# One signal of TensorE a pass, x transposed three pairs ahead, and evenly spaced indirect transfers in a recurrent mixture-of-experts kernel

## The reference

```python
x = L0_attn_x; xn = _layernorm(x)
# branch 1: recurrence, from a second layernorm of xn
u = xn2 @ Ws.T + bs + xn2 @ Wi.T + bi
h_t = tanh(h_{t-1} @ A.T + u_t)                     # a scan over 2048 steps
s = (H @ Wo.T + bo) * sigmoid(xn2 @ Wg.T + bg) + xn
# branch 2: top 4 of 16 experts, each silu(gate) * up, 256 -> 2*128 -> 256
scores = sigmoid(xn @ gate_w.T); idx = top_k(scores + gate_b, 4)
y = sum_k w_k * expert_k(xn) + shared_expert(xn)
out = x + s * silu(y)
```

## Time and profile before

| | |
|---|---|
| time, median of 3 runs | 443.7 us (442.36 to 444.87) |
| span of the profiled execution | 513.9 us |
| busy in it: PE, PEld | 339.1 us (66%), 261.7 us (51%) |
| busy in it: DVE, ACT, POOL | 311.1 us (61%), 251.0 us (49%), 265.4 us (52%) |
| moved by DMA | 109.27 MB, mean 213 GB/s |

### The profile page before, as it was taken

One profiled execution on the slowest core, in us unless ns is written; L12 is line 12 of the kernel. 1 busy time (PEld: TensorE's weight loads), 2 busy tenths in 40 slices (PEclk: granted clock), 3 DMA queues, 4 the chain that ended last, 5 costly groups with the idle time before them and its releaser, 6 DMA issues.

```text
span 513.9 us, 10001 instructions
## 1 busy us (share of the span) xinstructions
PE 339.1 (66%) x3107; PEld 261.7 (51%) x3107; DVE 311.1 (61%) x977; ACT 251.0 (49%) x462; POOL 265.4 (52%) x278
## 2 busy tenths in 40 slices
PE   0365566849467786976799968797876968645210
PEld 0352443626355665755698846575654756433100
DVE  4899776676703545545643626786776555346745
ACT  1851666536434455443787746565664644422000
POOL 2005377766646566655600165766555554436773
PEclk9976698797876889888999989999997898676555
DMA  7998499425443566654779768899977777436653
GB/s 247 305 328 281 129 343 331 161 86 201 143 165 127 175 186 201 196 172 156 216 220 269 227 192 268 281 282 285 285 243 211 249 217 225 128 119 194 174 160 126
DMA packets 88675, 109.27 MB, mean 213 GB/s; under 512 B 9649, under 2 KB 78002, under 8 KB 88626
## 3 DMA queue, kind: packets, MB, share of 16 engines
q1 hardware_dynamic: 74656, 74.47, 45.7%
q0 software_dynamic: 12288, 33.57, 20.7%
q10 hardware_dynamic: 1682, 0.59, 0.4%
HBM read 55.91 MB, written 52.69 MB: 211 GB/s over the span
## 4 chain that ended last, share of the span: by engine, by line
PE 35%; another core or an unknown queue 12%; issue 10%; ACT 8%; DVE 6%; POOL 5%; DMA 1%; ACTq 1%; POOLq 0%; DVEq 0%
PE bank L850 13%; PE bank L872 8%; PE bank L656 6%; POOL xn_parts L638 5%; PE bank L863 3%; ACT xn_f L1851 3%; PE bank L898 2%; ACT sh_h L1868 1%; ACT y_ring L1875 1%; ACT xn_f L1859 1%; ACT x_ring L1881 1%; PE bank L948 1%; DVE mix_sb L1371 1%; PE bank L774 1%
## 5 line engine op out<-in xcount | busy, mean ns | idle before, releaser
L638 POOL DMA_INDIRECT xn_parts<-y_slots,slot_u x128 | 127.2, 994 | 126.2 <-PE bank L656 39.6
L619 POOL DMA_INDIRECT x_slots<-xn_parts,slot_u x128 | 131.7, 1029 | 115.1 <-DVE slot_u L1253 36.0
L850 PE MATMUL bank<-w_all,xn_f 128*128 (+1 forms) x864 | 122.2, 295 | 22.2 <-issue 11.5
L850 PEld LDWEIGHTS bank<-w_all,xn_f 128*128 128x128 f16 x864 | 87.3, 106 | 44.8 <-issue 30.6
L1524 DVE SCALAR_TENSOR_TENSOR xn_f<-bank,xn_f 128x256 f32<-128x256 f32 x72 | 30.5, 424 | 111.9 <-ACT xn_f L1859 69.3
L1851 ACT ACTIVATE xn_f<-bank 128x1024 f16<-128x1024 f16 x72 | 73.5, 1022 | 36.7 <-remote 22.3
L872 PE MATMUL bank<-w_all,sh_silu 128*128 (+1 forms) x432 | 68.2, 299 | 5.5 <-ACT y_ring L1875 4.2
L1875 ACT ACTIVATE y_ring<-bank 128x512 f32<-128x512 f32 x72 | 42.9, 596 | 54.4 <-PE bank L872 33.7
L1859 ACT ACTIVATE xn_f<-bank 128x256 f32<-128x256 f32 x72 | 27.5, 382 | 55.0 <-remote 32.4
L656 PE MATMUL bank<-ident_h,w_stage 128*128 128x128 f16 x576 | 48.6, 231 | 1.5 <-issue 1.4
L872 PEld LDWEIGHTS bank<-w_all,sh_silu 128*128 128x128 f16 x432 | 41.8, 106 | 14.5 <-issue 7.5
(11 more groups left out here) (215 smaller groups left out, 456.9 us busy)
## 6 DMA issues: line engine op xcount, KB each, us to landing
w_stage<-x_slots SPq DMA_DIRECT2D x72, 256.0 KB
y_slots<-y_ring SPq DMA_DIRECT2D x72, 256.0 KB
x_slots<-zero_h SPq DMA_DIRECT2D x10, 1024.0 KB
x_ring<-in_x SPq DMA_DIRECT2D x32, 256.0 KB
w_stage<-in_w13t SPq DMA_DIRECT2D x17, 256.0 KB
x_ring<-in_x SPq DMA_DIRECT2D x8, 512.0 KB, 7.7
out<-mix_sb SPq DMA_DIRECT2D x15, 256.0 KB
w_stage<-in_w2t SPq DMA_DIRECT2D x17, 128.0 KB
```

What stands on the lines that cost most here:

```text
L619: eng.indirect_dma_start(out=x_slots, out_offset=bass.IndirectOffsetOnAxis(ap=slot_u[:, n * TOPK + k:n * TOPK + k + 1], axis=0), in_=xn_pa ...
L638: eng.indirect_dma_start(out=fin_y[:, r, j, k, :], out_offset=None, in_=y_slots[0:2 * READY_PAIR[c] * P, :], in_offset=bass.IndirectOffset ...
L850: mm = eng.matmul(gu[:, j * 2 * F:(j + 1) * 2 * F], xg_T[:, n % 2, ((j * 2 + px) * KD + k) * P:((j * 2 + px) * KD + k + 1) * P], weights_o ...
```

## The change

**Signals.** The signals `pair_t`, `pair_gu`, `pair_ht`, `pair_down`, `scan_mm` and `mix_mm` are gone. The last PE instruction of a pass gives the one signal `pair_pass`, and every engine that waited for a group now waits for the end of its pass (`passed_after`). The shared expert's second product keeps its own signal only in the tail.

**Order in a pass.** PE's pass n is now: first product of pair n+1, transposes of x of pair n+3, transposes of the hidden values of pair n-1, one step of the recurrence, second product of pair n-3. There are 75 passes. ACT and DVE start their pass n with what PE's pass n has finished. The recurrence takes passes 1 to 10 and 12 to 27, a step in each, with a shift in 11 and 28; check, fallback, parts and states move from slots 50, 54, 55 and 86 to 85, 90, 91 and 110, the mixing from slot 93 to slot 123. `UNIT_PAIR` has nine units, in passes 42 to 68, so units 9 to 15 come in the tail. SP loads six pairs ahead.

**Spacing.** In place of the half pairs, POOL writes a small tile (`spacer`, 128 x 128 fp16) before each of the scatters 61 to 127 and each gather of units 0 to 10 and waits for that write: 67 + 88 = 155 times. The gathers of units 11 to 15 have nothing between them.

```diff
-    XB_RING, YS_RING, AHEAD = 6, 5, 5
+    XB_RING, YS_RING, AHEAD = 6, 5, 6
+    X_AHEAD, H_BEHIND, DOWN_BEHIND = 3, 1, 3
...
-        SCAN0 = [6, 24]
-        SHIFT = {21: 0, 48: 1}
+        SCAN_PASS = (1, 2 + WARM)
+        SHIFT_PASS = tuple(first + steps for first, steps in zip(SCAN_PASS, STEPS))
...
-        UNIT_PAIR = tuple(40 + 10 * c // 3 for c in range(10))
+        UNIT_PAIR = tuple(42 + 10 * c // 3 for c in range(9))
...
-        MIX_SLOT = {93 + 6 * c: c for c in range(NU)}
+        MIX_SLOT = {123 + 6 * c: c for c in range(NU)}
...
+            def space(i):
+
+                eng.memset(spacer[:, :], 0.0).then_inc(spaced, 1)
+                eng.wait_ge(spaced, i + 1)
...
                 elif i >= HEAD_SCATTERS:
-                    half_pair(SCATTER_HALF + int((i - HEAD_SCATTERS) / PER_HALF_SCATTER))
+                    space(i - HEAD_SCATTERS)
...
-                    beside_gather(c * FT * TOPK + i)
+                    if c < NU - ROW_UNITS:
+                        space(TOPK * NT - HEAD_SCATTERS + c * FT * TOPK + i)
...
-            for n in range(NPAIR + 2):
-                if n + 2 < NPAIR:
-                    pair_x(n + 2)
+            for n in range(PASSES_OF_PAIRS):
                 beside(SLOTS * n)
                 if n + 1 < NPAIR:
-                    pair_up(n + 1)
+                    last = pair_up(n + 1)
                 beside(SLOTS * n + 1)
-                if 1 <= n <= NPAIR:
-                    pair_h(n - 1)
+                if n + X_AHEAD < NPAIR:
+                    last = pair_x(n + X_AHEAD)
+                if 0 <= n - H_BEHIND < NPAIR:
+                    last = pair_h(n - H_BEHIND)
                 beside(SLOTS * n + 2)
-                if n >= 2:
-                    pair_y_down(n - 2)
+                if (step := scan_place(n)) is not None and n > 1:
+                    last = scan_step(*step)
+                if n in SHIFT_PASS:
+                    scan_shift(SHIFT_PASS.index(n))
+                if n >= DOWN_BEHIND:
+                    last = pair_y_down(n - DOWN_BEHIND)
+                last.then_inc(pair_pass, 1)
```

More of the change, by code:

```diff
@@ L206, in recurrent_gated_moe @@
         zero_e = sb("zero_e", [P, E])
+        spacer = sb("spacer", [P, SPACER], f16)
         lnw_sb, lnb_sb = sb("lnw_sb", [P, KD]), sb("lnb_sb", [P, KD])
@@ L379, in recurrent_gated_moe, with mix_pass, scan_place @@
         UNIT_SLOT = {SLOTS * p: c for c, p in enumerate(UNIT_PAIR)}
-        MIX_SLOT = {93 + 6 * c: c for c in range(NU)}
+        MIX_SLOT = {123 + 6 * c: c for c in range(NU)}
         def mix_place(slot, offset):
             return MIX_SLOT.get(slot - offset)
-        def scan_place(slot):
+        def mix_pass(c):
+            return next(slot for slot, unit in MIX_SLOT.items() if unit == c) // SLOTS
+        def scan_place(n):
             for p in range(2):
-                at_ = slot - SCAN0[p]
-                if 0 <= at_ < STEPS[p] // 2 * 3 and at_ % 3 < 2:
-                    return p, at_ // 3 * 2 + at_ % 3
+                if 0 <= n - SCAN_PASS[p] < STEPS[p]:
+                    return p, n - SCAN_PASS[p]
             return None
@@ L834, in pair_x @@
                     eng.wait_ge(xT_lo, NB)
-                transposed(n % 2, lambda j: x_blk[:, xb_at(n), j // 4, (j % 4) * P:(j % 4 + 1) * P], 8, pair_t)
+                tb = TP[n % 2][:, :].bitcast(f16)
+                for j in range(8):
+                    t = eng.transpose(tb[:, j * P:(j + 1) * P], x_blk[:, xb_at(n), j // 4, (j % 4) * P:(j % 4 + 1) * P],
+                                      ident_h[:, :])
+                return t
             def pair_up(n):
@@ L959, in beside @@
                     experts(EXPERT_SLOT[slot])
-                if (place := scan_place(slot)) is not None:
-                    scan_step(*place)
-                if slot in SHIFT:
-                    scan_shift(SHIFT[slot])
-                if slot == CHECK:
+                if slot == FLAG:
                     scan_check()
@@ L974, in _ @@
             pair_x(0)
-            pair_x(1)
+            pair_x(1).then_inc(pair_pass, 1)
             eng.wait_ge(scored, NB)
@@ L1675, in _ @@
             pair_up(0)
-            for n in range(NPAIR + 2):
-                if (step := scan_place(SLOTS * n)) is not None:
+            pair_split(0)
+            for n in range(PASSES_OF_PAIRS):
+                beside(SLOTS * n)
+                if (step := scan_place(n)) is not None:
                     scan_sum(*step)
-                beside(SLOTS * n)
-                if (step := scan_place(SLOTS * n + 1)) is not None:
-                    scan_sum(*step)
+                if n in SHIFT_PASS:
+                    scan_shift(SHIFT_PASS.index(n))
+                if 0 <= n - H_BEHIND < NPAIR:
+                    pair_h(n - H_BEHIND)
                 if n + 1 < NPAIR:
                     pair_up(n + 1)
-                if n < NPAIR:
-                    pair_split(n)
+                    pair_split(n + 1)
                 beside(SLOTS * n + 1)
-                if 1 <= n <= NPAIR:
-                    pair_h(n - 1)
                 beside(SLOTS * n + 2)
@@ L1912, in _ @@
             pair_up(0)
-            for n in range(NPAIR + 2):
-                if n + 2 < NPAIR:
-                    pair_x(n + 2)
+            pair_x(2)
+            pair_split(0)
+            for n in range(PASSES_OF_PAIRS):
                 beside(SLOTS * n)
+                if n >= DOWN_BEHIND:
+                    pair_y_out(n - DOWN_BEHIND)
                 if n + 1 < NPAIR:
                     pair_up(n + 1)
-                if n < NPAIR:
-                    pair_split(n)
-                beside(SLOTS * n + 1)
+                if (step := scan_place(n)) is not None:
+                    beside(SLOTS * n + 1)
+                    scan_step(*step)
+                if n + X_AHEAD < NPAIR:
+                    pair_x(n + X_AHEAD)
+                if n + 1 < NPAIR:
+                    pair_split(n + 1)
+                if scan_place(n) is None:
+                    beside(SLOTS * n + 1)
                 beside(SLOTS * n + 2)
-                if n >= 2:
-                    pair_y_out(n - 2)
             for c in range(len(UNIT_PAIR) - 1, NU - 1):
```

98 lines of the change are left out of this document (45 added, 53 removed).

## The result

The changed kernel takes **488.6 us** (median of 4 runs, 488.13 to 489.44) against 443.7: ratio 1.103, 95% interval 1.100 to 1.106. It is slower by 44.8 us, inside the likeliest case's own range of 466 to 490.

What follows compares the result with a forecast made beforehand. POOL's chain of 256 transfers was taken to bound unprofiled runs. Spacers (14.7 us at scatters, 19.4 at gathers) and a later first gather took the sum from 441.0 to 482.3; 480 us forecast, range 424 to 490, likeliest 466 to 490.

Steps and rivals of the forecast that it cites:

- the likeliest case: Whole kernel: POOL's chain becomes longer by about 40 us, giving 466 to 490 us; chance 0.47.
- The late signals: PE's signals: late largely in profiled executions only; should mostly go, the span falling from 513.9 to about 482 us.
- The sum for before, 441.0: POOL's chain in the kernel before, rebuilt from its transfer times without late signals: 441.0 us against a median of 443.7.
- The spacer: POOL's write before 155 transfers: +0.22 us each, 14.7 us for the scatters and 19.4 for the gathers.
- Recurrence: Passes 21 to 27: one step a pass lengthens each by a product of 0.31 us, 2.1 us in all.
- To the first gather: Last scatter to gather 0, second product three passes behind: scatters end at 243.8, gather 0 at 291.2 against 269.
- The passes beside the gathers: Passes 35 to 74: 2.9, 3.5 and 2.8 us each, 134 us from 287.7, last product at 421.5.
- The product of unit 9: Tail: unit 9 multiplied by 429.5, before POOL needs it at 434.4, so covered by 5 us.
- Rival 2: Whole kernel: slower by less, spacer mostly hidden and the tail's product of unit 9 bounding, 450 to 466 us; chance 0.17.
- Rival 1: Whole kernel: faster, as late signals slow unprofiled runs too; 416 us, or 410 to 438; chance 0.30.
- Rival 3: Whole kernel: no change, late signals or half-pair pacing cost the runs as much as the spacer; 441 to 446; chance 0.06.
- Rival 4: PE's signals: one a pass as late as four, profiled span near 500, unprofiled time as forecast; inside that chance of 0.47.

Runs made afterwards that it cites:

- b_spacer: Kernel before with POOL's 155 spacers and the wait for each in place of the half pairs, all else untouched: 471.9 us, ratio 1.065.
- a4o_down2_flag: a_free with a4's signals, ACT's y copy and DVE's hidden copy later in the pass, second product two passes behind, PE's check later: 473.7 us.
- before_again: The kernel before, unchanged, profiled once more: span 440.4 us, where the first profiled execution had 513.9.
- b_free: Kernel before without any pacing of POOL, no half pairs and nothing in their place: 441.9 us, ratio 0.997.
- a4: a_free with each group of PE given its own signal again and the waits of the kernel before: 478.7 us, ratio 1.078.
- a_free: Changed kernel with its 155 spacers taken out and nothing in their place: 480.2 us, ratio 1.081 to the kernel before.
- b_write: b_spacer with POOL waiting only for the write before the one just issued: 449.9 us, ratio 1.016.
- b_scan1: b_free with the change's places for mixing and units and the recurrence at one step a pass: 450.2 us, ratio 1.018.

## Why the prediction was right, and where it was not

**The late signals.** Right that the runs are not so; the spans near the medians in both kernels (440.4 and 487.7) settle it. Right for a thinner reason than it seemed: I took the lateness for an effect of profiling on this kernel, which the spacer would cure. It was one execution.

**The sum for before, 441.0.** It hit 440.4 by three errors that cancel. Scatter 60 ended at 139.9 only in the disturbed execution, at 132.5 in the second profile and between 131.9 and 133.8 in all others. That is most of the 9.2 us by which I had the end of the scatters too late. From there to the first gather I had 40 us where 43.6 passed: the first pass after PE's wait of 8.34 us took 4.47 us (224.27 to 228.74) with most of PE's matmuls at half speed (12 of the first product in 2.77 us instead of 1.47; granted clock 0.83 for 220 to 240 us), and some of the passes beside the mixing took 3.90 and 3.06 us, where I had 2.64 for each. And the gathers are 1.332 apart, not 1.294, 4.9 us over 127. One of the marks by which I wanted to be judged, the last scatter after 235, failed for this reason (233.3). The distance between the kernels, 14.7 forecast and 13.5 measured, held.

**The spacer.** 0.22 us forecast, 0.19 to 0.20 measured, 1.46 between starts against 1.49 forecast. Between the bounds (nothing, and 0.53) the row on the 0.28 from a signal to a transfer was the right one to take; it stands again in the brackets of b_spacer's rows.

**Recurrence.** The step's product lengthened a dense pass from 2.64 to 2.84 us, 0.20, not 0.31. The sum lacked the check of the recurrence, which the change puts among the dense passes ahead of a first product: PE waited 2.96 us for it, until 265.02.

**To the first gather.** 47.4 us forecast (243.8 to 291.2), 52.1 measured, but 43.6 in before instead of 40: the difference is 8.5 where I had 7.4. The changed kernel has the half-speed pass too, 5.46 us from 237.86 to 243.32.

**The passes beside the gathers.** This step failed. I held them to 3.5 us by the DMA share, 0.91 in five passes of 3.80, and said that a pass can't be much under 3.5. Both numbers came from the disturbed execution. Undisturbed, before makes them in 3.32 at a share of 0.98, and the changed kernel needs 3.87 at 0.93 (both shares for 300 to 380 us): the transfers allow a shorter pass than it has. Nor is it the clock, granted at 0.96 there: a4o_down2_flag has 1.00 and still takes 3.78. I looked for what the order does to PE and costed each wait there, and left out what it does to the steps of DVE and ACT in these passes. There the time went, as far as the rows show: in 300 to 380 us DVE is busy for 63.75 and idle for 16.2, of which 15.4 for ACT; in before it is busy for 69.52 and waits 9.0 for ACT, in more passes. The product of unit 9 came at 438.9, not 429.5. POOL reached it when forecast (434.2, forecast 434.4), and what I had as covered by 5 us is a wait of 5.43 us.

**The rivals.** Rival 2 named the right second bound and underpriced it: the changed kernel with no spacer at all takes 480.2, where I had 463. So the total was right by a wrong split, and that is luck. I had 34 us for the spacers and 7 for the rest, as if they added; by themselves they cost 30.0 and 38.2 (480.2 less 441.9), and together 46.6 (488.6 less 441.9), since long passes and spaced gathers wait in parallel. Rival 1 fell with the result and before_again. Rival 3 fell with before_again, as for the late signals, and with b_free, as for the half pairs. Rival 4 fell with before_again: there was nothing late to cure.

**Signals.** a4 has its seven kinds of signals back and takes 1.5 us less than a_free, within what the runs differ. By the price of 26.3 ns an increment in the Trainium skill (TensorE: Matmul & The Clock Gate, the cost: per-tile semaphore tail), which is there for the tiles of one packed group of matmuls, three more a pass would be an estimate of 5.7 us more. No run here shows that, in dense passes or elsewhere; the runs of a_free and a4 spread over 4.6 and 4.3 us, so a part of it can't be ruled out.

## What to carry to other kernels

When a profiled span is far from the median of the runs, take the profile again before reading stretches from it: rates, shares and starting points all came from an execution that the runs never repeated. Price a slowdown by what remains when it is taken away, not only by what it adds: where two chains wait for each other at every unit, a stretch takes as long as the slower one, so 30 and 38 us made 47 and not 68. Where two engines in program order hand one pair's data back and forth within a pass, look for what each then waits for; the order of before, with the second step a pair behind, had no wait there.

## What the runs showed of the hardware that I had not expected

- One execution of a kernel had a span 73 us longer than the second profiled one (513.9 against 440.4), with half of TensorE's signals over 0.5 us late while the busy times of DVE, ACT and POOL stayed within 2% (311.1, 251.0 and 265.4 against 309.6, 252.0 and 269.2). It did not come back in the second profile, nor in any run.
- A small write of POOL between two indirect transfers costs 0.09 us from start to start though it lasts 0.22 (1.35 against 1.26, in b_write and b_free). Waiting for it costs 0.11 more (1.46, b_spacer).
- Two versions with nearly the same work in a pass (DVE busy 3.18 and 3.12 us) differ by 0.44 us a pass (3.34 and 3.78, b_scan1 and a4o_down2_flag) by the order of that work alone, transposes and loads of x ahead included.
- The first pass after TensorE had waited 8.34 us began at half speed: 12 matmuls in 2.77 us, where the next pass had 1.47 (before_again, 225.10 and 229.19 us).
